# A graph layer on one core: 20 of 80 edge chunks of a quad gathered by indirect DMA in place of 16, and 60 by one-hot products in place of 64

## The reference

```python
h_self = x @ W_lin + b_lin
messages = x[dst] @ W_msg + b_msg
msg_sum = segment_sum(messages, src, num_segments=n_nodes)
counts = segment_sum(ones, src, num_segments=n_nodes)
h_agg = msg_sum / maximum(counts, 1.0)[:, None]
h = concatenate([h_self, h_agg], axis=1) @ W_upd + b_upd
out = layernorm(x + relu(h))
```

## Time and profile before

| | |
|---|---|
| median of three runs | 1187.7 us (1186.47 to 1189.11) |
| the profiled execution | 1187.18 us |
| its span, first to last instruction | 1185.5 us |
| mean granted TensorE clock | 0.955 |
| busy: PE, DVE, ACT, POOL | 1063.7, 945.7, 765.5, 520.3 us |
| indirect gathers on POOL | 478 (400 chunks, 75 spills, 3 rare) |
| matmuls of the quads (L1306, L1319, L1332, L1344) | 7925, 6400, 1600, 600 |

### The profile page before, as it was taken

How to read it: one execution, slowest core, us unless ns; L and a number is a source line. 1 busy time by engine, 2 the same in 40 slices (tenths; PEclk the granted TensorE clock), 3 DMA queues, 4 the chain that set the end, 5 groups by cost and what they waited for, 6 DMA issues and landing times. The chain is left out here.

```text
span 1185.5 us, 52295 instructions
## 1 busy us (share of the span) xinstructions
PE 1063.7 (90%) x21321; PEld 962.6 (81%) x21321; DVE 945.7 (80%) x2190; ACT 765.5 (65%) x1827; POOL 520.3 (44%) x502
## 2 busy tenths in 40 slices
PE   1848989988878849999999999999999999999996
PEld 1838888878778739888889889889988899898885
DVE  7899999999999875777777777777777777777774
ACT  0312333332111129989999989999999999898994
POOL 3000000000000047776666667676677777676650
PEclk9978989989989759999999999999999999999998
DMA  9202323221143025443444443444444444444430
GB/s 119 81 32 95 125 78 116 95 91 50 50 130 94 3 70 122 119 120 111 111 111 112 114 110 111 111 111 111 111 114 113 112 111 111 111 112 110 111 84 19
DMA packets 122443, 116.29 MB, mean 98 GB/s; under 512 B 36442, under 2 KB 105047, under 8 KB 122134
## 3 DMA queue, kind: packets, MB, share of 16 engines
q1 hardware_dynamic: 96700, 64.96, 19.3%
q0 software_dynamic: 23024, 47.31, 15.5%
q10 hardware_dynamic: 2490, 0.67, 0.3%
HBM read 89.79 MB, written 23.10 MB: 95 GB/s over the span
## 5 line engine op out<-in xcount | busy, mean ns | idle before, releaser
L1306 PE MATMUL slot<-big 32*128 32x384 bf16 x7925 | 721.4, 323 | 9.2 <-DVE big L963 7.6
L587 ACT ACTIVATE big<-slot 128x384 bf16<-128x384 f32 x1600 | 662.9, 497 | 85.2 <-PE slot L1306 76.5
L1319 PE MATMUL acc<-big 32*128 32x385 bf16 x6400 | 689.6, 323 | 1.0 <-issue 0.8
L1306 PEld LDWEIGHTS slot<-big 32*128 32x128 bf16 x7925 | 471.6, 92 | 62.6 <-issue 11.3
L653 POOL DMA_INDIRECT big<-x,dst_at x400 | 427.9, 1070 | 187.7 <-issue 100.9
L1319 PEld LDWEIGHTS acc<-big 32*128 32x128 bf16 x6400 | 436.0, 93 | 22.3 <-issue 3.1
L1332 PE MATMUL acc<-big 32*128 32x385 bf16 x1600 | 352.1, 322 | 0.1
L975 DVE TENSOR_TENSOR big<-col_lo,iota_lo 128x512 bf16<-128x512 f16 x400 | 150.4, 418 | 160.3 <-PE acc L1319 151.5
L1344 PE MATMUL acc<-big 32*128 32x385 bf16 x600 | 192.8, 321 | 0.0
L647 POOL MEMSET big<- 128x8 bf16 x4 | 0.2, 100 | 412.8 <-issue 412.8
L963 DVE TENSOR_SCALAR big<-big,iota_k 128x2048 bf16<-128x2048 f16 (+8 forms) x225 | 160.2, 733 | 5.1 <-DMA big<-rows 3.8
(11 more groups left out here) (150 smaller groups left out, 832.7 us busy)
## 6 DMA issues: line engine op xcount, KB each, us to landing
big<-rows SPq DMA_DIRECT2D x100, 128.0 KB
x<-big SPq DMA_DIRECT2D x24, 384.0 KB, 2.6
big<-x,dst_at POOLq DMA_INDIRECT x400
big<-in_x SPq DMA_DIRECT2D x24, 256.0 KB, 3.1
base<-big SPq DMA_DIRECT2D x24, 256.0 KB, 2.5
big<-in_x SPq DMA_DIRECT2D x48, 128.0 KB
big<-base SPq DMA_DIRECT2D x48, 128.0 KB
out<-big SPq DMA_DIRECT2D x48, 128.0 KB
```

The costliest lines, as they stand in the source:

```text
L587: act.activation(xg[R % NX][:, i, 0:F3], slot[i // 2][:, i % 2, 0:F3], ACT.Copy).then_inc(s["xg_ready"], 1)
L1306: ins = nc.tensor.matmul(slot[lane // 2][:, lane % 2, 0:F3], W[q % NW_][rows, hot_at(g, k), :], xwin[rows, WIN_AT[g] + k, :], start=k == 0 ...
L1319: ins = nc.tensor.matmul(acc[lane][:, 0:F3 + 1], l_of(R, i)[rows, :], xg[R % NX][rows, i, 0:F3 + 1], start=r == 0 and i == 0, stop=last an ...
```

## The change

Chunks 60 to 63 of each quad are no longer fetched by products but gathered by DMA. So a quad has 15 runs and 10 pairs. The lists of runs after which pairs and spills are added are written anew, and since 15 is odd, `hot_nodes`, which fills `L` for two runs at once, now counts runs through quads: a pair of runs can belong to two quads, and the last one is alone.

```diff
-    CP = 64
+    CP = 60
     CD = C - CP
     RUNS = CP // 4
...
-        ORDER = [g for a in range(RUNS // 2) for g in (a + RUNS // 2, a)]
+        ORDER = [RUNS // 2] + [g for a in range(RUNS // 2) for g in (a + RUNS // 2 + 1, a)]
...
-        PAIR_RUNS, SPILL_RUNS = [4, 6, 8, 10, 11, 13, 15, 17], [5, 7, 9, 12, 14, 16]
+        PAIR_RUNS, SPILL_RUNS = [4, 5, 7, 8, 9, 11, 12, 13, 15, 16], [6, 8, 10, 12, 14, 16]
...
-        PAIR_NODES, WIN_FROM = [2, 5, 8, 11], 5
+        PAIR_NODES, WIN_FROM = [2, 4, 6, 9, 12], 5
...
                 def hot_nodes(P_):
-                    q, a = P_ // (RUNS // 2), P_ % (RUNS // 2)
                     if P_ >= NL:
                         dve.wait_ge(s["aggregated"], 2 * (P_ - NL + 1))
-                    for b in range(2):
-                        g = ORDER[2 * a + b]
+                    for b in range(min(2, Q * RUNS - 2 * P_)):
+                        q, r = divmod(2 * P_ + b, RUNS)
+                        g = ORDER[r]
...
-                        P_ = q * (RUNS // 2) + r // 2 + 2
+                        P_ = (q * RUNS + r) // 2 + 2
...
-                        if r % 2 == 0 and 2 < P_ < Q * (RUNS // 2):
+                        if (q * RUNS + r) % 2 == 0 and 2 < P_ < (Q * RUNS + 1) // 2:
                             hot_nodes(P_)
```

## The result

The changed kernel takes 1214.1 us (median of 4, 1211.4 to 1217.6) against 1187.5 us: a ratio of 1.0227, interval 1.0197 to 1.0257. It is slower, as forecast (1230, range 1201 to 1253), for the forecast reason, and by 26.7 us where 42.5 were expected. The profiled execution took 1211.89 us with a span of 1210.2 us.

The account below looks back on a forecast made before the run. PE sets the pace before, POOL's gathers after the change: start 427.0 plus 578 gathers at 1.36 us, less 0.3, gives 1212.8; 15.2 us tail and 1.7 us from span to time make 1229.7 us, range 1201 to 1253.

Parts of the forecast that it names:

- POOL's hidden load: On POOL before the change: 19 gathers with 0.30 us gaps need 26.0 of a quad's 29.3 us, leaving 3.3 us slack.
- POOL becomes the bound and never waits for PE: In the quads: 23 gathers need at least 28.6 us, above PE's 27.75, so POOL sets the pace without waiting.
- PE's gain of 39 us: In the quads: 625 matmuls for 661 would save 1.57 us in each of 25 quads, were PE still the bound.
- The forecast PE share of 89%: In the profile windows after the change: PE's busy share falls to about 89%, with L1332 waiting for the DMA queue.
- The pricing of PE by matmuls alone: PE's time in a quad taken as its number of matmuls times 44.4 ns: 625 give 27.75 us.
- The gather at 1.36 us: On POOL: each of 578 gathers takes 1.36 us including the 0.30 us gap, likely 1.31 to 1.40.
- the mean over all: On POOL before the change: all gathers average 1.367 us including the gap; the forecast chose a value near it.
- What stretches a gather: On POOL: a gather meeting a DVE operation with two SBUF inputs near its start waits for its end, then needs 0.82 us.
- Start and tail: Around the gathers: POOL starts at 427.0 us; after the last gather come 2.0 us transfer, 1.2 us PE, 12.0 us DVE.
- The cheap gather: Rival on POOL: gathers meet fewer two-input DVE operations, g falls below 1.287 us and the kernel is faster; chance 0.09.
- PE kept its clock: Answers a rival: PE loses clock in its new waits; at half of each quad slow, 1488 us; chance 0.02.
- rival 3: Longer DVE locks on POOL, from more fast-form window matrices or gathers in step: 1252.8 to 1264.4 us; chance 0.06.

Follow-up runs that it names:

- the run with 19 gathers: Changed kernel, but chunks 16 to 19 of the DMA side are gathered in the first quad only, PE's work unchanged: 1158.1 us, ratio 0.9774 to before.
- the kernel before with 23: Kernel before the change plus four gathers a quad into spare buffers that nobody reads, other engines' work untouched: 1222.2 us, ratio 1.031.
- 62 and 18 chunks: Split between the kernel before and the changed one: 62 chunks of a quad by products in 16 runs, 18 gathered by DMA: 1187.5 us, ratio 1.0015.
- the run without L: Changed kernel, but DVE makes the L matrices only for the first eight runs and later runs reuse them: 1194.6 us, ratio 1.0079.

## Why the prediction was right, point by point

- **What bounds the kernel now, and POOL's hidden load.** Right. The slack of 3.3 us a quad was all that POOL had; four gathers need 5.3.
- **POOL becomes the bound and never waits for PE.** Right: no wait over 0.3 us, and the run with 19 gathers and the kernel before with 23 show cause and cost each alone.
- **PE's gain of 39 us.** It is there, but smaller: 1185.0 to 1158.1 is 27 us, as a matmul takes 45.2 ns in place of 44.4 with the lighter quads. It is hidden behind POOL in the changed kernel. The forecast PE share of 89% was 92 to 95%. The pricing of PE by matmuls alone is the weak step: 62 and 18 chunks had 18 matmuls fewer in a quad and gained nothing.
- **The gather at 1.36 us.** The step that was mis-sized. Measured 1.332: 578 gathers took 1193.84 - 424.39 + 0.30 = 769.8 us for the 786.1 forecast, 16.3 us too much, all of it work rather than gap. The 1.322 of the first 60 gathers was nearer than the mean over all that I took. That mean held something that the change took away. In the kernel before 45 gathers take over 1.5 us, nearly two in each quad and 3.4 to 3.6 us apart, as the second and the fourth of the earlier trace rows; they make 39 of all 58 us of stretch. In the changed kernel there are 17, with 13 of 47 us. In the kernel before POOL waits for PE once in a quad and so meets the same operations of DVE in every quad; free of that wait, it meets them at changing moments. The counts are measured, this reason for them is argued.
- **What stretches a gather.** Right for operations with two SBUF inputs (1244 of 1266 gathers), but not the whole of it. The prediction put the 2.08 us of the gather at 712.65 down to the two L975 of the earlier trace rows. It starts inside this one, the fast form of L963, and both L975 follow:

```profile
712.50 0.74 DVE L963 TENSOR_SCALAR big<-big,iota_k 128x2048 bf16<-128x2048 f16 x1
```

- **Start and tail.** First gather at 424.39, 2.6 us earlier than the 427.0 taken over; other runs of the same program part begin between 424.2 and 427.6, so this is scatter. Last gather's end to the end of the span: 1210.2 - 1193.84 = 16.4 us, not 15.2: transfer and PE together 4.3 us to DVE's first step at 1198.17 (3.2 forecast), then 12.0 as forecast.
- The sum: 1229.7 - 16.3 - 2.6 + 1.2 = 1212.0, the profiled execution to 0.1 us; the median is 2.2 us above it.
- **Rivals.** The cheap gather didn't come (1.332 against the 1.287 from which it would decide). PE kept its clock (1.00 in all windows). The fast form of W does hold a gather (159 of 161), as rival 3 feared, and more shapes are fast than before (from 512 columns up, five for three). That it cost little was luck: gathers stood behind it for about 1.3 us, in the kernel before for about 9.9. The Trainium skill (SBUF — State Buffer, Who interferes with whom) says that a DVE instruction with two SBUF inputs contends with a GpSimd instruction that reads SBUF; the gathers at 717.02 and 719.74 agree. It also says that DVE in a two-port mode locks GpSimd out fully; no trace names a mode, but if the fast form is such a one, the traces agree: the gather at 532.62 of the run without L waited for its end.

## What to carry to other kernels

Add the fixed gap to every instruction of a queue before calling its engine half idle: 77% busy was full here. A transfer engine with slack takes more work for nothing until its period meets the bound's, then each item costs its full time, so move work in steps smaller than the slack; when the unit is too large for every pass, give it to some passes only (here that gained where taking it unevenly from the row groups in every pass gained nothing). Work on one engine can be paid for on another: what DVE did beside POOL changed the mean gather by up to 6%. A mean measured while an engine waits once in each pass goes with that pace and may change when the wait goes. And one instruction that overlaps another without delay proves little: sort all of them by what runs at their start.

## What the runs showed of the hardware

- Between two indirect gathers on POOL lie 0.30 us in all 13 kernels, with or without a wait between them.
- A gather of 128 rows takes 0.945 us. If it starts inside a DVE operation with two SBUF inputs (1244 of 1266) or inside the fast form of L963 (159 of 161), it ends 0.8 us or more after that operation's end: 0.81 to 0.83 us in the cases shown, later where more such operations follow, up to 2.88 us in all. Inside the slow form of L963 it is not held (1 of 323).
- The comparison of L963 takes 679 ns for 1792 columns, but 1206 for 1920. Its shapes of an even number of runs (by 128 columns) are fast, those of an odd number slow, from 512 to 2048 columns (1280 take 533 ns, 640 take 538); why was not tried.
